# All four units of transposed rows ahead of the down projection in the expert loop, instead of two ahead and two behind its first tile

## What is computed

```python
def _moe_forward(x, router_w, w1, w2, shared_gate_up, shared_down, shared_gate_w):
    logits = xf @ router_w
    probs = jax.nn.softmax(logits, axis=-1)
    topw, topi = jax.lax.top_k(probs, K)                     # K = 2 of E = 8 experts
    combine = zeros((n, E)).at[arange(n)[:, None], topi].add(topw)
    h = jax.nn.silu(jnp.einsum('nd,edf->nef', xf, w1))       # w1: 8 x 1024 x 1024
    ye = jnp.einsum('nef,efd->ned', h, w2)                   # w2: 8 x 1024 x 1024
    routed = jnp.einsum('ne,ned->nd', combine, ye)
    gu = xf @ shared_gate_up
    gate, up = (gu[:, :F], gu[:, F:])
    shared = jax.nn.silu(gate) * up @ shared_down
    shared = jax.nn.sigmoid(xf @ shared_gate_w) * shared
    return (routed + shared).reshape(b, t, d)
```

## Time and profile before

| | |
|---|---|
| runs | 1123.75, 1116.73, 1116.67 us; median 1116.73 |
| profiled execution | 1117.11 us, span 1115.3 us |
| TensorE busy | 1104.5 us, 99% of the span |
| VectorE busy | 638.5 us, 57% |
| ScalarE busy | 482.9 us, 43% |
| GpSimd busy | 67.9 us, 6% |
| DMA | 156.99 MB, mean 141 GB/s |

### The profile page before, as it was taken

How to read it: one execution, slowest core, us unless ns; L and a number is a source line. 1 busy time by engine, 2 the same in 40 slices (tenths; PEclk the granted TensorE clock), 3 DMA queues, 4 the chain that set the end, 5 groups by cost and what they waited for, 6 DMA issues and landing times.

```text
span 1115.3 us, 16113 instructions
## 1 busy us (share of the span) xinstructions
PE 1104.5 (99%) x6225; PEld 953.0 (85%) x6225; DVE 638.5 (57%) x805; ACT 482.9 (43%) x712; POOL 67.9 (6%) x88
## 2 busy tenths in 40 slices
PE   7999999999999999999999999999999999999998
PEld 5889998877777999878789999888988988988876
DVE  6798745776667744343373522445646556556545
ACT  4513321477888312211234222245655646555550
POOL 3000000000000000000000430200000000000003
PEclk9999999999999999999999999999999999999999
DMA  7222211232222022722004442367586676666647
GB/s 249 76 76 77 67 48 38 76 105 75 103 76 76 1 76 76 261 75 76 1 1 169 152 110 76 117 266 271 172 290 219 223 259 226 237 229 213 236 175 280
DMA packets 76485, 156.99 MB, mean 141 GB/s; under 512 B 7160, under 2 KB 7432, under 8 KB 76432
## 3 DMA queue, kind: packets, MB, share of 16 engines
q1 hardware_dynamic: 64908, 127.30, 33.3%
q10 hardware_dynamic: 7300, 15.41, 3.8%
q0 software_dynamic: 4224, 13.55, 3.8%
HBM read 135.69 MB, written 20.54 MB: 140 GB/s over the span
## 4 chain that ended last, share of the span: by engine, by line
PE 94%; DVE 2%; DMA 2%; issue 0%; DVEq 0%; POOL 0%; ACT 0%; POOLq 0%; SPq 0%; ACTq 0%
PE ps L1627 22%; PE ps L1629 22%; PE ps L1628 22%; PE ps L2038 10%; PE ps L2039 5%; PE ps L1726 2%; PE ps L1666 1%; PE ps L1712 1%; PE ps L1941 1%; PE ps L1942 1%; PE ps L1872 1%; PE ps L1873 1%; PE ps L1757 1%; DMA y_second<-expert_rows,slots 1%; DMA x_s<-in_x 1%; DVE x L1605 1%
## 5 line engine op out<-in xcount | busy, mean ns | idle before, releaser
L986 DVE TENSOR_TENSOR w_lo<-w_raw,w_hi 128x2048 fp32r<-128x2048 f32 x108 | 244.7, 2289 | 137.7 <-ACT w_hi L680 133.1
L680 ACT CAST w_hi<-w_raw 128x2048 fp32r<-128x2048 f32 x108 | 203.4, 1911 | 88.2 <-PE ps L1942 36.2
L2038 PE MATMUL ps<-xe,w_hi 128*128 128x448 f32 x512 | 160.9, 375 | 0.0
L2039 PE MATMUL ps<-xe,w_lo 128*128 128x224 f32 x512 | 134.8, 263 | 0.0
L2038 PEld LDWEIGHTS ps<-xe,w_hi 128*128 128x128 f32 x512 | 95.9, 187 | 7.9
L1627 PE MATMUL ps<-w_hi,he_hi 128*128 128x512 f32 (+1 forms) x256 | 101.2, 395 | 0.0
L1629 PE MATMUL ps<-w_hi,he_lo 128*128 128x512 f32 (+1 forms) x256 | 100.2, 391 | 0.0
L1628 PE MATMUL ps<-w_lo,he_hi 128*128 128x512 f32 (+1 forms) x256 | 100.0, 391 | 0.0
L2039 PEld LDWEIGHTS ps<-xe,w_lo 128*128 128x128 f32 x512 | 97.5, 190 | 0.4
L1627 PE MATMUL ps<-w_hi,xt_hi 128*128 128x512 f32 (+1 forms) x240 | 96.0, 400 | 0.1
L1629 PE MATMUL ps<-w_hi,xt_lo 128*128 128x512 f32 (+1 forms) x240 | 93.7, 391 | 0.0
(11 more groups left out here) (324 smaller groups left out, 2002.1 us busy)
## 6 DMA issues: line engine op xcount, KB each, us to landing
w_raw<-in_L_ffn_w SPq DMA_DIRECT2D x64, 1024.0 KB, 5.7
w_raw<-in_L_gnn_W_neigh SPq DMA_DIRECT2D x8, 1024.0 KB, 6.2
w_raw<-in_L_gnn_W_self SPq DMA_DIRECT2D x8, 1024.0 KB, 5.1
w_raw<-in_L_ffn_shared_gate_up SPq DMA_DIRECT2D x8, 1024.0 KB, 6.4
w_raw<-in_L_mix_Wv SPq DMA_DIRECT2D x4, 1024.0 KB, 6.4
w_raw<-in_L_mix_Wk SPq DMA_DIRECT2D x4, 1024.0 KB, 5.1
w_raw<-in_L_mix_Wq SPq DMA_DIRECT2D x4, 1024.0 KB, 5.0
w_raw<-in_L_mix_Wo SPq DMA_DIRECT2D x4, 1024.0 KB, 5.0
```

The source lines that it names most:

```text
L680: copy(w_hi[b][:, s * HK:(s + 1) * HK, :], w_raw[s][:, :, :]).then_inc(hi_done, 1)
L986: V_.tensor_tensor(w_lo[b][:, k, :], w_raw[s][:, :, :], as32(w_hi[b][:, k, :]), ALU.subtract).then_inc(lo_done, 1)
L2038: mat(PS(key)[:, a, 0:2 * B], wh[:, k, w_cols], xe[:, :, k, 0:B], start=k == 0, stop=False)
L2039: last = mat(PS(key)[:, a, 0:B], wl[:, k, w_cols], xe_hi[:, k, 0:B], start=False, stop=k == KF - 1)
```

## The change

FIRST takes all four pairs and LATER is empty. By the same two names the units' places in the ring and the programs of three engines follow.

```diff
@@ -141,7 +141,7 @@
     place = {key: n for n, key in enumerate(units)}
 
     ROWS = [(s, f) for s in range(BC) for f in range(2)]
-    FIRST, LATER = ROWS[:2], ROWS[2:]
+    FIRST, LATER = ROWS, []
     block_units = ([("he", n) for n in range(KF // 2)] + [("xe+", s, f) for s, f in FIRST]
                    + [("y", 0, 0)] + [("xe+", s, f) for s, f in LATER]
                    + [("y", h, s) for h in range(2) for s in range(BC)][1:])
```

## The result

The changed kernel takes 1156.64 us (median of four runs, 1155.97 to 1159.27) against 1116.7 before: ratio 1.0348, 95% interval 1.0322 to 1.0374, so 3.5% slower by that ratio, and 40 us by the medians. The forecast was 1141 with a range to 1149. The profiled execution took 1157.09 us, with a span of 1155.3.

The account below looks back on a forecast made before the run. TensorE was taken to bound the kernel, carrying 94% of the chain of waits and busy throughout each block. Eight blocks at 2.99 us add 23.9 us to 1117.1, clock and moved work nothing: 1141 us, range 1137 to 1149.

Parts of the forecast that it names:

- Parts 1 and 2: At y(0,0) in each block: tile handed back late, 3.66 us, less 0.67 us given back: 2.99 us per block.
- the 0.11 us of way: From the end of VectorE's subtraction for the first transposed unit to TensorE's start of y(0,0): 0.11 us.
- the 0.67 us that y(0,0) gives back: Between y(0,0) and y(0,1): eight transposes leave, 0.61 us, and a slower matmul behind them, 0.06 us.
- the two waits and their releasers: TensorE waits per block, released by VectorE: about 0.7 us at the last transposed unit, 2.1 us at y(0,0).
- I take zero, and 2.0 us per block as the upper end: Clock cost of the 4.4 us per block holding only transposes and waiting: zero, at most 2.0 us.
- rival (a): The clock falls in some or all blocks, 1 to 8 restarts of 2.0 us: 1143 to 1157 us; chance 0.20.
- the pace at the program's start: Nineteen matmuls after 4.77 us without work took 5.30 us, against 3.3 at the later pace: restart costs 2.0 us.
- the twin: Ahead of the loop: sixteen transposes, then a shared-branch tile taking the first transposed tile; 2.1 us stretch, clock 1.00 behind.
- Part 3: Moved casts, subtractions and gather trigger: weight work ends 0.9 us later, slack 4.3 us at third y tile, cost nothing.
- Rival (d): Moved weight work comes too late for y(1,0) or the next block: 1145 us or more; chance 0.03.
- (b): No slowdown: hand-back to y(0,0) not late, blocks save under 0.1 us each: 1116 to 1117 us; chance 0.03.
- (c): The wait at y(0,0) is smaller, 1 to 2.6 us a block: 1125 to 1138 us; chance 0.08.

Follow-up runs that it names:

- evacuation as before with filling: Changed kernel, last two transposed units evacuated behind the weight work as before the change, plus eight unused matmuls per block in the wait at y(0,0): 1140.78 us.
- the same without filling: Changed kernel, with ScalarE and VectorE evacuating the last two transposed units behind the weight work, as before the change; no added matmuls: 1155.52 us.
- Three ahead: Changed kernel with three transposed units ahead of y(0,0) and the fourth behind it: 1124.86 us, ratio 1.0063.
- early evacuation: Changed kernel, last two transposed units evacuated behind the weight work, the first cast and subtracted ahead of the last hidden unit's Silu: 1129.03 us.
- two-tile kernel: Changed kernel with both halves of a transposed group in one PSUM tile, y tiles taking the tiles of hidden units 2 and 3: 1149.73 us.
- the two-tile kernel with the old evacuation: Two-tile kernel, with ScalarE and VectorE evacuating the second transposed group behind the weight work, as before the change: 1117.43 us, ratio 1.0008.
- filled with transposes: Changed kernel with seventeen extra transposes per block between the last transposed unit and y(0,0): 1146.8 us.
- early evacuation with the gather later: Changed kernel, gather waiting for the end of y(0,1), first transposed unit cast and subtracted ahead of the last hidden unit's Silu: 1144.14 us.
- two-tile kernel with the gather later: Two-tile kernel with GpSimd's gather also waiting for the end of y(0,1)'s matmuls: 1132.14 us.
- the filling: Changed kernel with eight unused 512-column matmuls per block in the wait at y(0,0): 1145.94 us, ratio 1.0254.
- the later gather: GpSimd's next gather also waits for the end of y(0,1)'s matmuls; on the changed kernel: 1169.97 us.

## Why the prediction was wrong

By medians, the 39.7 us (1156.64 - 1116.98; against the 1116.7 measured beside it, 39.9) split like this:

| term | forecast | measured | from |
|---|---|---|---|
| hand-back of the tile for y(0,0) | 23.9 | 23.8 | evacuation as before with filling, 1140.78 - 1116.98 |
| fallen clock | 0 | 14.7 | the same without filling, 1155.52 - 1140.78 |
| moved evacuation, weight loads, gather | 0 | 1.1 | changed kernel, 1156.64 - 1155.52, not clear of the noise of four runs each |

The middle term takes in what the blocks of nearly 50 us cost beyond the others.

**Parts 1 and 2, right.** The chain from the last hidden unit to the tile's release, the 0.11 us of way, the 0.67 us that y(0,0) gives back, the two waits and their releasers: 2.98 us a block against 2.99. Three ahead, early evacuation and the two-tile kernel with the old evacuation moved the time as the same chain says.

**The clock, where the forecast failed.** The step is "I take zero, and 2.0 us per block as the upper end", with rival (a) at one chance in five and cut off at about four restarts. The price was near, 14.7 / 8 = 1.84 us a block against 2.0 (1.6 in most blocks, 48.18 against 46.57), and in part by luck: it came from the pace at the program's start, 0.28 us from one matmul to the next, and the window from 5 to 10 us there has a granted clock of 1.00, so that row shows no fall of the clock. The frequency was wrong: it fell in eight blocks of eight.

The reason given for zero was that the longest single wait, 2.1 us, is near the twin. That compares unlike things: 2.06 us is the twin's whole stretch, transposes and all, and TensorE waited 0.36 us of it. Like with like, the forecast had two waits of 2.8 us together in 4.4, the run has 2.51 (0.59 + 1.92) in 4.43, and no row had such a case. The runs add these:

| run | between ordinary matmuls | waits of it | clock |
|---|---|---|---|
| changed kernel, the six blocks of 48 us | 4.42 or 4.43 us | 0.59 + 1.92 us | falls in each |
| filled with transposes, first block | 4.43 us | 0.58 us | stays |
| three ahead, first block | 2.70 us | 1.33 us | stays |
| early evacuation, rest as before | 2.87 us | 0.59 + 0.36 us | stays |

So the length of the stretch does not decide it: the second row has the first one's, and its clock stays. The early evacuation shortened stretch and waits together and can't tell them apart. Nor is it alike in all blocks, though each is the same program. Over the whole loop a wait of 1.85 us, mostly with 0.3 to 0.4 more behind it, was followed by a fall six times of seven (early evacuation with the gather later), and in the two-tile kernel with the gather later a wait of 1.78 us was and one of 1.96 was not. The rows on record allowed (a) more than one chance in five, but did not make it certain.

**Part 3, right in sum and wrong in reason.** Moving two casts, two subtractions and a trigger cost 1.1 us here, which can't be told from the forecast's nothing. The slacks that I worked out were for a TensorE that is 3 us late, and took the loads at 5.7 us. Where TensorE is not late (two tiles), the same edit costs 32 us, with a load of 10.1 to 10.4 us in each block. I had checked the subtractions of y(1,s), which have 4 us; of the next block's first weights I said only that the later tile hides the later load, and gave the load its old length. Rival (d) named this mechanism, with a chance of 0.03; it was at work, in two blocks of the changed kernel visibly and else under the cover of the larger loss. With the filling that cover is thinner, and it costs 5.2 us (1145.94 - 1140.78).

**Rivals (b) and (c)** did not occur. (b)'s other half, that bunching by itself gains nothing, holds: 1117.43.

What stays open: why the later gather helps the two-tile kernel by 17.6 us and costs the changed one 13.3. The traces show that loads and gather then meet differently, but no run separates which load it is. Also what, beside the waits, decides whether the clock falls, and why it stays low for longer in two of the blocks. No run beat the kernel before; the nearest was even with it.

## What to carry to other kernels

Where tiles of a ring are taken in turn, moving a unit changes who waits for whose evacuation: list for each claim the unit four places earlier and where that unit's release stands in the queues of the evacuating engines, behind what. Price an idle stretch of TensorE at its length and then once more for the clock; add up all waits that stand close together, and compare them with the waits of a known row and its whole stretch with the whole stretch. Where no row has such a case, give the fall a real share in the forecast, as a repeated loop pays it in every pass. And a slack worked out under a delay holds only as long as the delay: if the wait is removed later, check the streams that it had covered.

## What the runs showed of the hardware

- Granted clock at 0.50 in all eight blocks of the changed kernel, in six of them with 4.4 us of transposes and waits (0.59 and 1.92 us); 1.00 throughout with 2.87 us (0.59 and 0.36), and 1.00 in the 4.43 us in which seventeen transposes filled the 1.92. Where ordinary matmuls stood on both sides, it fell behind all seven waits of 2.2 to 3.3 us (two-tile kernel). The matmuls of 512 columns came 0.43 us apart at the low level and 0.23 at the high one.
- Extra work made the kernel faster: eight unused matmuls a block took it from 1156.64 to 1145.94 us, and from 1155.52 to 1140.78 with the old evacuation. Seventeen transposes did nearly as well, 1146.8.
- A weight load of 1 MB took 10.09 to 10.35 us beside a gather and the other load, once in each of seven blocks of the two-tile kernel, where 5.7 is the median of the kernel before.
- GpSimd's two small copies took 2.38 us instead of 0.30 where they met VectorE's weight subtractions, and a gather's issue 2.08 instead of 0.98; VectorE's subtractions kept their 2.29 us each:

```profile
810.11 2.38 POOL L642 COPY idx<-cols 128x1 uint32 x2 [41.57 <-DVE xe L992]
813.43 2.08 POOL L645 DMA_INDIRECT xg<-xn_rows,idx  x1 [0.94 <-issue]
```
